# Attention of layers 1 to 3: the low parts of the turned probabilities before the maximum, and layer 2's queries in four pieces

## The chip, the cores and the metric

One core of one Trainium2 chip runs the whole program as one launch. The metric is the time of one execution in microseconds (us), the median of several runs. Engines are named as in the profile: PE (TensorE matmuls), PEld (its weight loads), DVE (VectorE), ACT (ScalarE), POOL (GpSimd), SP (SyncE).

## The reference, cut to what matters

The program is four layers of cross attention and a feed-forward network on x (1024 tokens of width 256, in 4 batches of 256) with a context of 4 x 512 keys of width 128. The change touches the attention of layers 1, 2 and 3 alone. Each has 16 heads of width 128. Of layer 1:

```python
q = (hidden_states @ Wq).reshape(B, Sq, H, D)
k = (encoder_hidden_states @ Wk).reshape(B, Skv, H, D)
v = (encoder_hidden_states @ Wv).reshape(B, Skv, H, D)
q = rmsnorm(q, gq)
k = rmsnorm(k, gk)
scores = jnp.einsum('bqhd,bkhd->bhqk', q, k) * scale
attn = jax.nn.softmax(scores, axis=-1)
out = jnp.einsum('bhqk,bkhd->bqhd', attn, v)
out = out.reshape(B, Sq, H * D)
return out @ Wo
```

Layers 2 and 3 are the same without the two norms; two heads share a key and a value head there, and a mask of the keys is applied. The result is added to x.

## The kernel before, in words

`heads_stage` (line 417) is called three times: "l1a" with `qk_norm` (layer 1), "l2a" with `made` (layer 2) and "l3a" (layer 3). Every product of full precision is made of three matmuls of fp32r operands: each operand is kept as a high part (rounded) and a low part (the difference), and high x high, high x low and low x high are added in PSUM (`product`, lines 565 to 569).

The head's weights are folded first: a = Wq Wk (so that the "queries" of a head are a times the normalised tokens, and the scores are those times the context), and wvo = Wv Wo. So each head is prepared in the pieces of `pieces` (line 435): "a", "q0" and "q1" (the queries of 512 tokens each, six matmuls of 512 columns) and "wvo". In layers 1 and 3, PE multiplies a and wvo too, and ACT copies them from a bank; in layer 2 (`made`) these products were made earlier and lie in SBUF, so that PE prepares q0 and q1 alone. ACT copies a piece out of its bank (line 669), POOL makes its high part (line 813) and its low part (line 817), from the second head on; for the first head ACT and DVE do it (lines 664 to 669 and 717).

The work of a head is four pairs, one for each batch; a pair is two units of 128 queries by 512 keys. There are 64 pairs in a layer. Each engine has its own queue in program order, and all of them go through `walk` (line 493): step k of an engine does one part each of several pairs. After the first head's preparation come eight steps written out, a hardware loop of six turns with eight steps each, eight more steps written out, and four steps that drain. In one step:

- PE: the scores of pair k (S: 6 matmuls of 512 columns, lines 608 to 620), the values of pair k-3 (V: 12 of 256 columns, lines 621 to 628), the output product of pair k-4 (Y: 6 of 256 columns, lines 629 to 640), one piece of the next head (`after`, line 641), then the turning of the probabilities of pair k-1 (T: 8 transposes, lines 643 to 650). In `walk` step k of a head prepares `pieces[k % 4]`, so a head's steps are: a, q0, q1, wvo.
- ACT: H, the high parts of pair k-2's turned probabilities, for its two units (line 676); E, the exponentials of pair k's two units with their sums (line 685); O, the high part of pair k-3's output (line 693 or 695); the copy of the piece (line 669).
- DVE: M, for each unit of pair k the mask (or the norm of the keys) with the maximum and the shift made of it (lines 732 to 748); the reciprocal of pair k-4's sums (line 753); L, the low parts of pair k-2's turned probabilities, two units (line 759); Olow, the low part of pair k-3's output (line 766 or 768); X, the two additions of pair k-4 to x (line 775).
- POOL: high and low parts of the next head's piece.
- SP loads weights in layers 1 and 3; in layer 2 it does nothing in the loop.

The banks: two for scores, two for turned probabilities (one per unit), one for the output, one for y, two for pieces. What sets the order around the change are these waits. H of a unit waits for T of that unit. L waits for H of the same unit (`high_done`). T of the next pair's unit waits for L (`turn_kept`), since it writes the same bank. E waits for M's shift (`shift_done`). O stands behind E in ACT's queue and waits for V. Olow waits for O (`o_high_done`). The next V waits for Olow (`o_kept`), and Y waits for X of the pair before (`x_added`), since each has one bank. X waits for Y. S of a unit waits for the maximum of the last pair's unit (`top_done`). The last steps of DVE's queue in one step, before:

```python
dve.reciprocal(inverse[:, at:at + 2], ...).then_inc(inverse_done, 1)
if exists(pair, 2):
    for q in range(2):
        dve.wait_ge(high_done, pair * 2 + (q - 3))
        dve.tensor_tensor(prob_low[part], turn_bank[q][:]..., prob_high[part]..., ALU.subtract).then_inc(turn_kept, 1)
if exists(pair, 3):
    dve.wait_ge(o_high_done, pair - 2)
```

Of the kernel before, what the change touches and what calls it, by code (L numbers as in the profile page):

```python
# [14 lines left out]
F32 = mybir.dt.float32  # L15
# [4 lines left out]
P = 128  # L20
BATCH = 4
# [395 lines left out]
def heads_stage(nc, m, dram, name, qk_norm, made=False):  # L417
# [16 lines left out]
    scale = float(P) ** -0.5  # L434
    pieces = ["a", "q0", "q1", "wvo"]
    n_pieces = len(pieces)
    on_bank = ["q0", "q1"] if made else pieces
    n_banked = len(on_bank)
    with Stage(nc, m, name) as st:
        if not made:  # L440
# [41 lines left out]
        if not qk_norm:  # L482
            norm.banks = turn_bank
        rms_loaded = st.sems("rms_loaded0", "rms_loaded1")
        (side_loaded, scores_ready, top_done, shift_done, exp_done, inverse_done, turn_ready,
         high_done, turn_kept, pv_ready, o_high_done, o_kept, own_high, split_done, y_ready, x_added, prep_ready,
# [3 lines left out]
            "x_added", "prep_ready", "prep_kept")  # L490
        set_up, gained, q_scale_done, first_high = st.sems("set_up", "gained", "q_scale_done", "first_high")

        def walk(engine, prepare, step, normalise=None):

            def two_heads(i, last=False):
                for k in range(2 * BATCH):
                    after, ahead = [pieces[k % BATCH]], k // BATCH + 1
                    if last and ahead == 2:  # L500
                        after = []
                    head = (i * 2 + k // BATCH, i, k // BATCH)
                    following = (i * 2 + ahead, i + ahead // 2, ahead % 2)
                    step(i * (2 * BATCH) + k, k, head, after, following)

            for piece in pieces:
                if piece == "q0" and normalise:
                    normalise(engine)
                prepare(piece, (0, 0, 0))
            two_heads(0)  # L510
            with engine.Fori(1, HEADS // 2 - 1) as i:
                two_heads(i)
            two_heads(HEADS // 2 - 1, True)
            for k in range(AHEAD):
                step(PAIRS + k, k, None, [], None)

        def is_head(h, number):
            return isinstance(h, int) and h == number

        parts_of = {"a": (a_high, a_low, a_h), "q0": (q_high, q_low, q_t), "q1": (q_high, q_low, q_t),  # L520
                    "wvo": (wvo_high, wvo_low, wvo)}

        def place(piece, slot):

            first, end = (int(piece[1]) * BANK, (int(piece[1]) + 1) * BANK) if piece in ("q0", "q1") else (0, D)
            return (slice(None), slot, slice(first, end)), end - first
# [7 lines left out]
        def exists(pair, back):  # L534

            return not isinstance(pair, int) or 0 <= pair - back < PAIRS

        with st.block() as block:
# [25 lines left out]
            def _(pe):  # L564
# [10 lines left out]
                def prepare(piece, head):  # L575
                    h, turn, slot = head
                    if piece not in on_bank:
                        return
                    n = on_bank.index(piece)
                    if piece == "a":  # L580
                        pe.wait_ge(w_loaded[slot], turn * 64 + 64)
                        if qk_norm:
                            pe.wait_ge(gained, h + 1)
                    bank = prep_bank[n % 2]
                    if is_head(h, 0):
                        wait_for(pe, split_done, 0 if made else n - 1)
                    elif is_head(h, 1) and n < 2:
                        pe.wait_ge(split_done, (2 if made else n_pieces - 1) + n)
# [17 lines left out]
                def step(pair, k, head, after, following):  # L606
# [22 lines left out]
                    if exists(pair, 4):  # L629
                        pe.wait_ge(o_kept, pair - 3)  # L630
                        wait_for(pe, x_added, pair * 2 - 8)
                        if k % BATCH == 0:
                            h = HEADS if head is None else head[0]
                            pe.wait_ge(split_done, h * n_pieces)
                        old = (k - 4) // BATCH % 2
# [4 lines left out]
                        last.then_inc(y_ready, 1)  # L640
                    for piece in after:
                        prepare(piece, following)
# [12 lines left out]
            def _(act):  # L655
# [14 lines left out]

                def step(pair, k, head, after, following):
                    if exists(pair, 2):
# [15 lines left out]
                    if exists(pair, 3):  # L688
# [8 lines left out]
                        last.then_inc(o_high_done, 1)  # L697
                    for piece in after:
                        prepare(piece, following)
# [4 lines left out]
            def _(dve):  # L704
                def prepare(piece, head):
                    h, turn, slot = head
                    if is_head(h, 0):
# [9 lines left out]
                        dve.tensor_tensor(low[at], of, high[at].bitcast(F32), ALU.subtract).then_inc(split_done, 1)  # L717

# [5 lines left out]

                def step(pair, k, head, after, following):
                    b = k % BATCH
                    if exists(pair, 0):
                        h, turn, slot = head
# [20 lines left out]
                    if exists(pair, 4):  # L749
# [37 lines left out]
            def _(pool):  # L787
# [9 lines left out]
                def prepare(piece, head):  # L797
                    h, turn, slot = head
                    if not is_head(h, 0):
                        number = h * n_pieces + pieces.index(piece)  # L800
                        high, low, whole = parts_of[piece]
                        at, _ = place(piece, slot)
                        if is_head(h, 1) and piece == "a":
                            pool.wait_ge(split_done, n_pieces)
                        if piece in on_bank:
# [6 lines left out]
                        pool.tensor_tensor(pool_woken[:], m.ones[:, 0:1], m.ones[:, 0:1], ALU.mult)  # L812
                        pool.tensor_copy(high[at], of).then_inc(own_high, 1)
                        pool.wait_ge(own_high, number + (1 - n_pieces))
                        if piece not in on_bank:
                            pool.tensor_tensor(second_woken[:], m.ones[:, 0:1], m.ones[:, 0:1], ALU.mult)
                        pool.tensor_tensor(low[at], of, high[at].bitcast(F32), ALU.subtract).then_inc(split_done, 1)
# [3 lines left out]
                def step(pair, k, head, after, following):  # L821
                    for piece in after:
                        prepare(piece, following)
# [2133 lines left out]
```

## Time and profile before

| | |
|---|---|
| median of 3 runs | 2414.33 us (2414.1 to 2418.16) |
| the profiled execution | 2415.74 us; its span is 2413.4 us |
| PE busy | 2119.8 us, 88% of the span |
| DVE busy | 1580.7 us, 65% |
| ACT busy | 1219.2 us, 51% |
| POOL busy | 777.2 us, 32% |
| mean granted TensorE clock | 0.913 of full speed |

The units of layer 1 run from 594.4 us of the span to 927.5, those of layer 2 from 1042.3 to 1370.9, those of layer 3 from 1829.4 to 2162.1 (first and last start of the operation of line 737); the drain of a layer follows. A busy share is a mean over stages with different limits; matmuls are pipelined, so that the durations of neighbouring ones overlap and their spacing is to be read from their starts. The profiled execution is 1.4 us above the median of the runs.

### The profile page before, as it was taken

How to read it: one execution, taken by the hardware profiler on the slowest of the kernel's cores; microseconds unless marked ns; L12 is line 12 of the kernel's file. 1: busy time of each engine (PE TensorE's matmuls, PEld its weight loads, DVE VectorE, ACT ScalarE, POOL GpSimd, SP SyncE). 2: the span in 40 equal slices, each digit the busy share in tenths (PEclk: the TensorE clock that was granted, in tenths of full speed). 3: DMA queues.
4: the chain of work that ended last, by engine and by line, in shares of the span. 5: the costliest groups of instructions: out<-in, count | busy, mean ns of one | idle time of the engine just before them, and what ended most of it. 6: DMA issues, size and time to landing. Idle time of an engine off the chain costs nothing. (4 is left out here: it accounts for less than half of the span.)

```text
span 2413.4 us, 42918 instructions
## 1 busy us (share of the span) xinstructions
PE 2119.8 (88%) x12471; PEld 1755.9 (73%) x12471; DVE 1580.7 (65%) x4466; ACT 1219.2 (51%) x3007; POOL 777.2 (32%) x1150
## 2 busy tenths in 40 slices
PE   5699978598999997789999978887868999996999
PEld 3555556476899995478888867777756999995887
DVE  6687858784777786577778863111236887885655
ACT  4788842274666664356666512222215666662333
POOL 3433312210333331123323156666632323311221
PEclk9777789799999998889999978998898999997999
DMA  1156020101211113100000026766761000004431
GB/s 62 43 112 188 0 88 1 64 2 44 73 72 60 60 66 106 39 4 1 0 0 0 5 82 195 204 203 188 210 218 32 16 20 20 20 1 109 118 110 50
DMA packets 132850, 174.01 MB, mean 72 GB/s; under 512 B 43820, under 2 KB 99092, under 8 KB 130040
## 3 DMA queue, kind: packets, MB, share of 16 engines
q1 hardware_dynamic: 121656, 140.27, 20.0%
q0 software_dynamic: 10656, 29.11, 3.9%
q10 hardware_dynamic: 416, 3.15, 0.3%
q8 instruction: 59, 0.97, 0.2%
q14 instruction: 63, 0.52, 0.1%
HBM read 155.57 MB, written 36.83 MB: 80 GB/s over the span
## 5 line engine op out<-in xcount | busy, mean ns | idle before, releaser
L2475 DVE COPY l2f_x_t<-bank 128x256 f32<-128x256 f32 x111 | 46.9, 424 | 269.3 <-PE bank L2205 132.2
L685 ACT ACTIVATE l1a_prob<-l1a_masked,l1a_shift,l1a_q_scale 128x512 f32<-128x512 f32 x128 | 104.4, 816 | 79.4 <-DVE l1a_shift L743 78.4
L2350 POOL DMA_INDIRECT l2f_x_rows_of<-l2f_x_rows,l2f_table x111 | 107.9, 972 | 88.9 <-remote 34.7
L2217 PE MATMUL bank<-l2f_x_t,l2f_w 128*128 128x128 f32 x888 | 128.4, 292 | 6.3 <-issue 6.0
L685 ACT ACTIVATE l2a_prob<-l2a_masked,l2a_shift 128x512 f32<-128x512 f32 x128 | 92.7, 724 | 81.1 <-DVE l2a_shift L747 78.3
L685 ACT ACTIVATE l3a_prob<-l3a_masked,l3a_shift 128x512 f32<-128x512 f32 x128 | 92.7, 724 | 80.3 <-DVE l3a_shift L747 77.6
L2306 ACT ACTIVATE l2f_h<-bank 128x128 f32<-128x128 f32 x111 | 30.8, 277 | 198.2 <-PE bank L2217 106.0
L2217 PEld LDWEIGHTS bank<-l2f_x_t,l2f_w 128*128 128x128 f32 x888 | 118.7, 208 | 9.2 <-issue 9.0
L2225 PE MATMUL bank<-l2f_w,l2f_h 128*128 128x256 f32 x222 | 77.1, 432 | 53.8 <-ACT l2f_h L2307 36.8
L1236 ACT ACTIVATE l0a_prob<-bank,l0a_shift 128x496 f32<-128x496 f32 (+1 forms) x256 | 122.6, 552 | 2.4 <-DVE l0a_shift L1260 2.3
L2355 POOL DMA_INDIRECT l2f_y_rows<-l2f_y,l2f_target x111 | 110.3, 994 | 37.5 <-issue 32.8
L1255 DVE TENSOR_REDUCE l0a_top<-bank 128x1 f32<-128x496 f32 (+1 forms) x256 | 90.2, 411 | 36.3 <-PE bank L1194 36.1
L737 DVE CUSTOM_DVE_ANT_0 l3a_masked<-bank,l3a_side 128x512 f32<-128x512 f32 x128 | 88.4, 691 | 18.0 <-issue 18.0
L737 DVE CUSTOM_DVE_ANT_0 l1a_masked<-bank,l1a_side 128x512 f32<-128x512 f32 x128 | 88.4, 691 | 15.0 <-issue 14.9
L737 DVE CUSTOM_DVE_ANT_0 l2a_masked<-bank,l2a_side 128x512 f32<-128x512 f32 x128 | 88.4, 691 | 12.6 <-issue 12.6
L2557 POOL TENSOR_TENSOR l3f_low<-l3f_raw,l3f_high 128x768 fp32r<-128x768 f32 x24 | 44.3, 1847 | 160.2 <-ACT l3f_high L2552 160.2
L1214 PEld LDWEIGHTS bank<-ident,l0a_prob 128*128 128x128 f32 x512 | 68.7, 167 | 30.5 <-issue 18.6
L1214 PE MATMUL bank<-ident,l0a_prob 128*128 128x128 f32 x512 | 87.8, 325 | 1.0 <-DVE l0a_prob L1269 0.3
L812 POOL TENSOR_TENSOR l3a_pool_woken<-ones 128x1 f32<-128x1 f32 x60 | 11.6, 193 | 231.2 <-ACT l3a_q_t L669 123.1
L2776 DVE TENSOR_TENSOR l3f_upped<-l3f_gate,bank 128x512 f32<-128x512 f32 x48 | 33.0, 688 | 77.7 <-PE bank L2677 69.7
L1194 PE MATMUL bank<-l0a_k_t,l0a_q_t 64*128 64x512 f32 x128 | 65.1, 567 | 21.1 <-ACT l0a_prob L1236 15.5
L812 POOL TENSOR_TENSOR l2a_pool_woken<-ones 128x1 f32<-128x1 f32 x60 | 11.6, 193 | 219.4 <-ACT l2a_q_t L669 183.3
(591 smaller groups left out, 7560.7 us busy)
## 6 DMA issues: line engine op xcount, KB each, us to landing
l2f_w<-w_rows SPq DMA_DIRECT2D x111, 304.0 KB
l1a_side<-rms SPq DMA_DIRECT2D x16, 1024.0 KB, 4.8
w_rows<-in_l2f_w SPq DMA_DIRECT2D x4, 2048.0 KB
l2f_hots<-l2f_y_rows SPq DMA_DIRECT2D x8, 768.0 KB, 10.0
l3f_raw<-in_l3f_w SPq DMA_DIRECT2D x24, 256.0 KB, 3.8
l3f_mix<-shares SPq DMA_DIRECT2D x16, 384.0 KB, 3.7
l2f_w_rest<-in_l2f_w SPq DMA_DIRECT2D x111, 48.0 KB
w_rows<-in_l2f_w SPq DMA_DIRECT2D x8, 512.0 KB
```

The lines of the kernel that those rows point to most:

```text
L685: act.activation(prob[:, unit, :], masked[:, unit, :], ACT.Exp, bias=shift[:, unit:unit + 1], scale=q_scale[:, slot, t:t + 1] if qk_norm e ...
L737: dve.tensor_tensor_reduce(masked[:, unit, :], score_bank[q][:], side[:, slot if qk_norm else 0, b * KEYS:(b + 1) * KEYS], 1.0, LOWEST, AL ...
L1194: pe.matmul(score_bank[k % 2 * 2 + q][:], q_t[rows, slot, q * P:(q + 1) * P], k_t[rows, slot, :], start=True, stop=True).then_inc(scores_r ...
L1214: last = pe.transpose(turn_bank[q][:, n * P:(n + 1) * P], prob[:, (k - 3) % 4, q, n * P:(n + 1) * P], m.ident[:])
L1236: last = act.activation(prob[:, at, q, first:end], score_bank[at % 2 * 2 + q][:, first:end], ACT.Exp, bias=shift[:, at, q, part:part + 1], ...
L1255: last = dve.tensor_reduce(top[:, at, q, part:part + 1], score_bank[k % 2 * 2 + q][:, first:end], AX_X, ALU.max)
L2217: last = pe.matmul(pair_bank[b % 2][:, n * P:(n + 1) * P], w[:, slot, first:first + P], x_t[:, b % 2, c * P:(c + 1) * P], start=(c == 0), ...
L2225: pe.matmul(y_bank[b % 2][:, 0:D], h[:, b % 2, 0, :], w[:, slot, DC * of.WIDTH:of.ROW], start=True, stop=False)
L2350: pool.indirect_dma_start(x_rows_of[:, b % of.X_SLOTS, :], None, x_rows, bass.IndirectOffsetOnAxis(table[:, b:b + 1], 0)).then_inc(gathere ...
L2355: pool.indirect_dma_start(y_rows, bass.IndirectOffsetOnAxis(target[:, b:b + 1], 0), y[:, b % of.Y_SLOTS, :], None).then_inc(y_stored[b % o ...
L2475: dve.tensor_copy(x_t[:, b % 2, :], turn_bank[b % 2][:, 0:D]).then_inc(x_kept, 1)
L2557: pool.tensor_tensor(self.low[:, slot, at], self.raw[:, slot, at], self.high[:, slot, at].bitcast(F32), ALU.subtract).then_inc(self.low_do ...
```

## The change

It does two things, in `heads_stage` alone.

1. All three layers: in DVE's step, L (lines 755 to 760) moves from behind the reciprocal to the head of the step, before M. So DVE's order is L, M, reciprocal, Olow, X. The queues of the other engines keep their order.
2. Layer 2 alone: the queries of a head are made in four pieces of 256 tokens (q0 to q3, each six matmuls of 256 columns), one in each of the head's four steps, in place of two of 512 in the middle two. wvo comes behind q3 in the fourth step, and "a" of the head after the next behind that, on POOL; "a" has its own semaphores (`a_done`, `own_a`). Before the first step "a" of head 1 is prepared too. PE's scores wait for the quarter that they read.

```diff
-    pieces = ["a", "q0", "q1", "wvo"]
+    queries = ["q0", "q1", "q2", "q3"] if made else ["q0", "q1"]
+    per_query = TOKENS // len(queries)
+    pieces = ["a"] + queries + ["wvo"]
     n_pieces = len(pieces)
-    on_bank = ["q0", "q1"] if made else pieces
+    on_bank = queries if made else pieces
+    due = [["q0"], ["q1"], ["q2"], ["q3", "wvo"]] if made else [[piece] for piece in pieces]
     n_banked = len(on_bank)
+    n_split = n_pieces - 1 if made else n_pieces
...
                 for k in range(2 * BATCH):
-                    after, ahead = [pieces[k % BATCH]], k // BATCH + 1
-                    if last and ahead == 2:
-                        after = []
+                    ahead = k // BATCH + 1
                     head = (i * 2 + k // BATCH, i, k // BATCH)
                     following = (i * 2 + ahead, i + ahead // 2, ahead % 2)
-                    step(i * (2 * BATCH) + k, k, head, after, following)
+                    after = [] if last and ahead == 2 else [(piece, following) for piece in due[k % BATCH]]
+                    if made and k % BATCH == BATCH - 1 and not last:
+                        after.append(("a", (i * 2 + ahead + 1, i + (ahead + 1) // 2, (ahead + 1) % 2)))
+                    step(i * (2 * BATCH) + k, k, head, after)
...
                 prepare(piece, (0, 0, 0))
+            if made:
+                prepare("a", (1, 0, 1))
...
-                    elif piece in ("q0", "q1"):
+                    elif piece in queries:
                         chunk = int(piece[1])
-                        pe.wait_ge(split_done, h * n_pieces + 1)
+                        if made:
+                            pe.wait_ge(a_done, h + 1)
+                        else:
+                            pe.wait_ge(split_done, h * n_pieces + 1)
                         for c in range(DC):
-                            last = product(bank[:], [of[:, slot, c * P:(c + 1) * P] for of in (a_high, a_low)],
-                                           [of[:, c, chunk * BANK:(chunk + 1) * BANK] for of in (m.x_high, m.x_low)],
+                            last = product(bank[:, 0:per_query], [of[:, slot, c * P:(c + 1) * P] for of in (a_high, a_low)],
+                                           [of[:, c, chunk * per_query:(chunk + 1) * per_query] for of in (m.x_high, m.x_low)],
                                            c == 0, c == DC - 1)
...
-                        if b % 2 == 0:
+                        if made:
+                            pe.wait_ge(split_done, h * n_split + (b + 1))
+                        elif b % 2 == 0:
                             pe.wait_ge(split_done, h * n_pieces + (2 + b // 2))
...
                     b = k % BATCH
+                    if exists(pair, 2):
+                        for q in range(2):
+                            dve.wait_ge(high_done, pair * 2 + (q - 3))
+                            part = (slice(None), k % 2, slice(None), slice(q * P, (q + 1) * P))
+                            dve.tensor_tensor(prob_low[part], turn_bank[q][:].rearrange("p (n t) -> p n t", n=KT),
+                                              prob_high[part].bitcast(F32), ALU.subtract).then_inc(turn_kept, 1)
                     if exists(pair, 0):
...
                         dve.reciprocal(inverse[:, at:at + 2], total[:, (k - 4) % 8 * 2:(k - 4) % 8 * 2 + 2]
                                        ).then_inc(inverse_done, 1)
-                    if exists(pair, 2):
-                        for q in range(2):
-                            dve.wait_ge(high_done, pair * 2 + (q - 3))
-                            part = (slice(None), k % 2, slice(None), slice(q * P, (q + 1) * P))
-                            dve.tensor_tensor(prob_low[part], turn_bank[q][:].rearrange("p (n t) -> p n t", n=KT),
-                                              prob_high[part].bitcast(F32), ALU.subtract).then_inc(turn_kept, 1)
...
                     if not is_head(h, 0):
-                        number = h * n_pieces + pieces.index(piece)
+                        if made and piece == "a":
+                            own, done, number = own_a, a_done, h
+                        else:
+                            own, done, number = own_high, split_done, h * n_split + (pieces.index(piece) - (n_pieces - n_split))
```

## Rows read from the trace of the kernel before

**Rows 1.** The page, busy time and share of the span.
```profile
PE 2119.8 (88%) x12471; PEld 1755.9 (73%) x12471; DVE 1580.7 (65%) x4466; ACT 1219.2 (51%) x3007; POOL 777.2 (32%) x1150
```

**Rows 2.** Windows: us; busy PE, PEld, DVE, ACT, POOL; clock, DMA share, GB/s.
```profile
640.00:880.00 240.00, 239.81 (x1635) 217.01 (x1635) 192.26 (x626) 158.43 (x359) 78.05 (x155) 1.00 0.19 66
1090.00:1330.00 240.00, 236.35 (x1564) 207.89 (x1563) 192.51 (x625) 149.75 (x337) 75.33 (x156) 1.00 0.00 0
```

**Rows 3.** Line 736, two per pair: three loops, layer 2's last pairs.
```profile
L736 DVE MEMSET l1a_woken<- x97: 59/59/59, 634.1 to 891.6; 128x1 f32 x97
L736 DVE MEMSET l2a_woken<- x97: 59/59/59, 1077.7 to 1335.6; 128x1 f32 x97
L736 DVE MEMSET l3a_woken<- x97: 59/59/59, 1869.0 to 2126.0; 128x1 f32 x97
L736 DVE MEMSET l2a_woken<- x15: 59/59/59, 1335.6 to 1370.0; 128x1 f32 x15
```

**Rows 4.** Timeline, layer 2, PE: start us, duration us. A pair with queries.
```profile
1194.90 0.48 PE L567 MATMUL bank<-ctx_t_high,l2a_q_high 128*128 128x512 f32 x1
...
1196.37 0.28 PE L567 MATMUL bank<-l2a_prob_high,ctx_high 128*128 128x256 f32 x1
...
1198.49 0.39 PE L567 MATMUL bank<-l2n_x_high,l2a_a_high 128*128 128x512 f32 x1
...
1199.89 1.04 PE L648 MATMUL bank<-ident,l2a_prob 128*128 128x128 f32 x8
...
1200.68 0.48 PE L567 MATMUL bank<-ctx_t_high,l2a_q_high 128*128 128x512 f32 x1
```

**Rows 5.** Timeline, layer 2, PE: the start of the second pair without queries.
```profile
1205.83 0.50 PE L567 MATMUL bank<-ctx_t_high,l2a_q_high 128*128 128x512 f32 x1
```

**Rows 6.** Timeline, layer 2, DVE and ACT, the step that starts at 1190.22 us.
```profile
1190.22 0.06 DVE L736 MEMSET l2a_woken<- 128x1 f32 x1 [0.39 <-PE bank L569]
...
1192.18 0.72 ACT L685 ACTIVATE l2a_prob<-l2a_masked,l2a_shift 128x512 f32<-128x512 f32 x1 [0.18 <-DVE l2a_shift L747]
...
1192.26 1.27 DVE L759 TENSOR_TENSOR l2a_prob_low<-bank,l2a_prob_high 128x512 fp32r<-128x512 f32 x2
...
1192.90 0.46 ACT L695 ACTIVATE l2a_o_high<-bank,l2a_valid 128x256 fp32r<-128x256 f32 x1
...
1193.44 0.47 DVE L768 SCALAR_TENSOR_TENSOR l2a_o_low<-bank,l2a_valid,l2a_o_high 128x256 fp32r<-128x256 f32 x1
...
1193.84 0.86 DVE L776 SCALAR_TENSOR_TENSOR x<-bank,l2a_inverse,x 128x256 f32<-128x256 f32 x2
...
1194.31 0.59 ACT L669 COPY l2a_q_t<-bank 128x512 f32<-128x512 f32 x1 [0.95 <-PE bank L569]
...
1194.79 1.08 ACT L676 CAST l2a_prob_high<-bank 128x512 fp32r<-128x512 f32 x2
```

**Rows 7.** Timeline, layer 1, DVE and ACT, the step that starts at 703.27 us.
```profile
703.27 0.06 DVE L736 MEMSET l1a_woken<- 128x1 f32 x1 [0.46 <-PE bank L569]
...
706.05 0.35 ACT L693 CAST l1a_o_high<-bank 128x256 fp32r<-128x256 f32 x1
...
706.82 0.86 DVE L776 SCALAR_TENSOR_TENSOR x<-bank,l1a_inverse,x 128x256 f32<-128x256 f32 x2
```

**Rows 8.** Timeline, layer 2, DVE and ACT, a step written out, then the drain.
```profile
1365.43 0.69 DVE L737 CUSTOM_DVE_ANT_0 l2a_masked<-bank,l2a_side 128x512 f32<-128x512 f32 x1 [0.28 <-issue]
...
1367.95 0.46 ACT L695 ACTIVATE l2a_o_high<-bank,l2a_valid 128x256 fp32r<-128x256 f32 x1
...
1375.32 0.47 ACT L695 ACTIVATE l2a_o_high<-bank,l2a_valid 128x256 fp32r<-128x256 f32 x1 [0.88 <-PE bank L569]
...
1375.83 0.48 DVE L768 SCALAR_TENSOR_TENSOR l2a_o_low<-bank,l2a_valid,l2a_o_high 128x256 fp32r<-128x256 f32 x1 [0.29 <-ACT l2a_o_high L695]
```

**Rows 9.** Timeline, layer 2, POOL: the first of wvo, the last of a.
```profile
1204.51 0.19 POOL L812 TENSOR_TENSOR l2a_pool_woken<-ones 128x1 f32<-128x1 f32 x1 [1.65 <-PE bank L569]
...
1206.70 0.74 POOL L817 TENSOR_TENSOR l2a_a_low<-products,l2a_a_high 128x256 fp32r<-128x256 f32 x1
```

More of the change, by code:

```diff
@@ L490, in heads_stage @@
             "x_added", "prep_ready", "prep_kept")
-        set_up, gained, q_scale_done, first_high = st.sems("set_up", "gained", "q_scale_done", "first_high")
+        set_up, gained, q_scale_done, first_high, a_done = st.sems("set_up", "gained", "q_scale_done", "first_high", "a_done")
         def walk(engine, prepare, step, normalise=None):
@@ L514, in walk @@
             for k in range(AHEAD):
-                step(PAIRS + k, k, None, [], None)
+                step(PAIRS + k, k, None, [])
         def is_head(h, number):
             return isinstance(h, int) and h == number
-        parts_of = {"a": (a_high, a_low, a_h), "q0": (q_high, q_low, q_t), "q1": (q_high, q_low, q_t),
-                    "wvo": (wvo_high, wvo_low, wvo)}
+        parts_of = {"a": (a_high, a_low, a_h), "wvo": (wvo_high, wvo_low, wvo)} | {q: (q_high, q_low, q_t) for q in queries}
         def place(piece, slot):
-            first, end = (int(piece[1]) * BANK, (int(piece[1]) + 1) * BANK) if piece in ("q0", "q1") else (0, D)
+            first, end = (int(piece[1]) * per_query, (int(piece[1]) + 1) * per_query) if piece in queries else (0, D)
             return (slice(None), slot, slice(first, end)), end - first
@@ L585, in prepare @@
                     if is_head(h, 0):
-                        wait_for(pe, split_done, 0 if made else n - 1)
+                        wait_for(pe, split_done, n - 1)
                     elif is_head(h, 1) and n < 2:
-                        pe.wait_ge(split_done, (2 if made else n_pieces - 1) + n)
+                        pe.wait_ge(split_done, n_banked - 1 + n)
                     else:
@@ L604, in prepare, with step @@
                     last.then_inc(prep_ready, 1)
-                def step(pair, k, head, after, following):
+                def step(pair, k, head, after):
                     b = k % BATCH
@@ L640, in step @@
                         last.then_inc(y_ready, 1)
-                    for piece in after:
+                    for piece, following in after:
                         prepare(piece, following)
@@ L669, in prepare, with step @@
                     act.copy((high if is_head(h, 0) else whole)[at], bank[:, 0:width]).then_inc(prep_kept, 1)
-                def step(pair, k, head, after, following):
+                def step(pair, k, head, after):
                     if exists(pair, 2):
@@ L697, in step @@
                         last.then_inc(o_high_done, 1)
-                    for piece in after:
+                    for piece, following in after:
                         prepare(piece, following)
@@ L716, in prepare @@
                             of = of_products(piece, h)
-                        dve.tensor_tensor(low[at], of, high[at].bitcast(F32), ALU.subtract).then_inc(split_done, 1)
+                        dve.tensor_tensor(low[at], of, high[at].bitcast(F32), ALU.subtract).then_inc(
+                            a_done if made and piece == "a" else split_done, 1)
                 def set_up_masks(dve):
@@ L723, in set_up_masks, with step @@
                                       ALU.max).then_inc(set_up, 1)
-                def step(pair, k, head, after, following):
+                def step(pair, k, head, after):
                     b = k % BATCH
+                    if exists(pair, 2):
[4 more added lines that the diff above has]
+                                              prob_high[part].bitcast(F32), ALU.subtract).then_inc(turn_kept, 1)
                     if exists(pair, 0):
@@ L799, in prepare @@
                     if not is_head(h, 0):
-                        number = h * n_pieces + pieces.index(piece)
+                        if made and piece == "a":
+                            own, done, number = own_a, a_done, h
+                        else:
+                            own, done, number = own_high, split_done, h * n_split + (pieces.index(piece) - (n_pieces - n_split))
                         high, low, whole = parts_of[piece]
                         at, _ = place(piece, slot)
-                        if is_head(h, 1) and piece == "a":
-                            pool.wait_ge(split_done, n_pieces)
+                        if is_head(h, 1) and piece == ("q0" if made else "a"):
+                            pool.wait_ge(split_done, n_split)
+                        if is_head(h, 1) and piece == "a" and made:
+                            pool.wait_ge(a_done, 1)
                         if piece in on_bank:
@@ L812, in prepare, with step @@
                         pool.tensor_tensor(pool_woken[:], m.ones[:, 0:1], m.ones[:, 0:1], ALU.mult)
-                        pool.tensor_copy(high[at], of).then_inc(own_high, 1)
-                        pool.wait_ge(own_high, number + (1 - n_pieces))
+                        pool.tensor_copy(high[at], of).then_inc(own, 1)
+                        pool.wait_ge(own, number if made and piece == "a" else number + (1 - n_split))
                         if piece not in on_bank:
                             pool.tensor_tensor(second_woken[:], m.ones[:, 0:1], m.ones[:, 0:1], ALU.mult)
-                        pool.tensor_tensor(low[at], of, high[at].bitcast(F32), ALU.subtract).then_inc(split_done, 1)
+                        pool.tensor_tensor(low[at], of, high[at].bitcast(F32), ALU.subtract).then_inc(done, 1)
                     if qk_norm and piece == "wvo" and not is_head(h, HEADS - 1):
                         gain_weights(h + 1, turn + slot, 1 - slot)
-                def step(pair, k, head, after, following):
-                    for piece in after:
+                def step(pair, k, head, after):
+                    for piece, following in after:
                         prepare(piece, following)
```

3 lines of the change are left out of this document (2 added, 1 removed).

## The prediction

> **What bounds the kernel now.** The page comes first: PE is busy for 88% of the span, more than any other engine [rows 1], but that is a mean over many stages, so I cut out two stretches of the changed stage. In layer 1 PE is busy for 239.81 of 240 us; in layer 2 for 236.35 of 240, DVE for 192.51 and ACT for 149.75 [rows 2], with the granted clock at 1.00, the upper of PE's two levels (2.4 GHz), throughout. So layers 1 and 3 are PE's, and layer 2 is PE's with 3.65 us per 240 left open. The spacing of line 736 gives the pace: 48 pairs take 257.5, 257.9 and 257.0 us in the loops of layers 1, 2 and 3, that is 5.365, 5.373 and 5.354 us a pair, and the last seven spacings of layer 2 take 34.4 us, 4.91 each [rows 3].
>
> PE's queue says what a pair must cost in layer 2. S takes 1.47 us, V and Y together 2.12 (18 matmuls of 256 columns, 0.118 each), Q, six matmuls of 512 columns, 1.40 (0.233 each), T 0.79: 5.78 with queries [rows 4], 4.38 without. The pair without queries that starts at 1200.68 takes 5.15 [rows 4, 5], since there T waits for L, and L stands behind M. That ring (S, M, L, T, S) is what the change takes away, and the spread of the queries evens the load: (2 x 5.78 + 2 x 4.38) / 4 = 5.08 us of PE a pair. Were PE the bound, this would be the pace of layer 2.
>
> **Part 1, L moved ahead of M: what it uncovers.** Nothing is added; every DVE operation stays, so what counts is what each stood beside. In the step at 1190.22 DVE's M ends where the second E starts, 1192.18 (E is released by the shift); E runs 0.72, and O starts as it ends, 1192.90, back to back: ACT's queue holds O behind E. O ends at 1193.36, Olow starts at 1193.44, and L stood from 1192.26 to 1193.44 exactly in this gap [rows 6]. So L's 1.18 us was free: DVE had work while ACT made E and O. After the change nothing but the reciprocal lies between M and Olow. DVE must wait for E and O in every step, and L is paid in front. This is a new ring inside one step, on two queues in program order: L, M, E, O, Olow, X, then the next step's L.
>
> Its length in layer 2's loop, by [rows 6]: L 1.18 (1192.26 to 1193.44); M with the second E and O up to O's end 3.14 (1190.22 to 1193.36); DVE's start after O 0.04 (in the drain, where Olow waits alone, O ends at 1375.79 and Olow starts at 1375.83 [rows 8]); Olow 0.40; X 0.86. The sum is 5.62. Where one DVE operation follows another directly they overlap by some 0.09 (L would end at 1193.53, Olow starts at 1193.44), and X before L is such a seam: 5.53 to 5.62, and I take 5.58, layer 3 alike. In layer 1 O is shorter: 703.27 to O's end at 706.40 is 3.13, plus 0.04; Olow and X end at 707.68, and X starts at 706.82, so X is 0.86; Olow to X I take as 0.33 to 0.40; with L 1.18 that is 5.54 to 5.61, less the seam: 5.45 to 5.61, and I take 5.51, as Olow has no scale there [rows 7]. In the steps written out M and E are closer: 1365.43 to 1368.41 is 2.98, against 3.14; ring 5.44, layer 1 5.37 [rows 8].
>
> Does anything else lengthen it? PE: V of the next pair waits for Olow, so it can start 0.9 before X ends. PE then needs 1.40 for V, 0.71 for Y, at most 1.40 for Q and 0.79 for T, so T ends about 3.5 us after L's start, while H, which waits for T, stands behind O on ACT at 4.4: not late. S is ready some 2 us before M asks for it. A pair with queries needs 5.78 on PE, 0.2 to 0.3 over the ring; two in a row slip by 0.6 at most, which that slack covers, and the pairs without queries give it back. ACT: after O it copies the piece (0.48 to its successor) and runs the first H (0.54), 1.02 in all, against 1.26 of Olow and X on DVE [rows 6], so L finds H done. So the ring sets the pace alone, and it is longer than the mean pace of all three layers.
>
> Sum of part 1 and the loops: layer 1 (5.51 - 5.365) x 48 = 7.0; layer 2 (5.58 - 5.373) x 48 = 9.9; layer 3 (5.58 - 5.354) x 48 = 10.8. The last seven spacings: layer 2 7 x 5.44 - 34.4 = 3.7; the others, whose last steps carry the same pairs, an estimate of 2.5 and 2.9. The first eight: O and X are only just coming in, and four full spacings at 5.44 stand against about 5.3; with L's first delay of M (under 1.2, I take 0.8) that is 1.0, 1.8 and 1.3. Together 40.9.
>
> **Part 2, four quarters in layer 2.** PE's columns stay the same: 24 matmuls of 256 columns a head at 0.118 are 2.83 us, 12 of 512 at 0.233 are 2.80 [rows 4]. So I cost the cut at nothing, and beneath the ring PE has 0.5 us a pair open besides. The Trainium skill, TensorE: Matmul & The Clock Gate, section "Back-to-back issue gap", speaks against the cut: it gives a sustained spacing of about 81 ns at 128 columns and 131 ns at 512, which between them makes some 98 ns at 256 (an estimate from that page), so that a head's 24 would cost 2.35 us and the 12 only 1.57, 0.8 more a head and 12 us in the layer, if PE bounds. The rows of 0.233 and 0.118 do not bear it out: here the cost goes by the column. ACT and POOL have two more fixed costs a head, both beside slack. At the start DVE's masks stand in front of the first quarter's low part, and two more pieces follow through two banks: bounded by nothing and by two pieces of 0.7, I take 0.8.
>
> One new wait: "a" now follows q3 and wvo on POOL, and PE's first quarter of the next step waits for it. wvo and a take 2.93 us (1204.51 to 1207.44 [rows 9]), a quarter half of that, so a is done 4.4 us after ACT's copy. In the ring's time that is about 3.5 into the next step, where PE would like it at 1.3: PE stands 2 us, T ends near 5, and the first H starts about when ACT is free. I cost it at nothing, at most 0.3 x 15 = 4.5.
>
> **Sum.** 40.9 + 0.8 = 41.7. The profiled execution took 2415.74, of which the span is 2413.4, so it would take 2457; it stands 1.4 over the median of the runs, 2414.33, and from that I predict 2456.
>
> **The rivals.**
>
> *PE stays the bound, and it gets faster.* If the step's ring were under 5.08, the old ring's loss in layer 2 would be gained: (5.373 - 5.08) x 48 = 14, with the ends 15, and layers 1 and 3, where PE has no gap, stay: 2399. For it: PE's shares [rows 2], and that T no longer waits for L. Against it: E and O leave Olow no way past them, and the ring would have to lose 0.5 us. It decides at a ring of 5.37, which is 0.21 below mine. Chance 0.05.
>
> *It comes out even.* A ring near 5.37, so that both sides cancel to within 0.2% of the time (5 us, about what a measurement can tell from no change here): the seams between operations would have to be three times what I see. Chance 0.04.
>
> *Lockstep.* PE's slips are not given back: V waits for Olow and M for S, so that each pair costs the larger of PE and the ring. Then 28 pairs with queries in layer 1 and 28 in layer 3, at 5.78, add 0.27 x 28 + 0.20 x 28 = 13; the loop's turns, and POOL's "a", another 5 each at most: 2470 to 2480. For it: one bank each for output and y. Against it: the slack counted above. Chance 0.15.
>
> *The forecast,* the ring alone, 0.76. Slower by over 0.2% holds forecast and lockstep: 0.91. The range: the ring at its lower ends, 0.06 a pair over 180 pairs, is 11 us less, and a little for ends that cost nothing: 2440. At the top it takes in lockstep and POOL's wait: 2480.
>
> **What the profile after would show.** Right: DVE idle before Olow by 1.1 to 1.2 us in nearly every step, released by ACT's O, 180 times, over 200 us in all; L with no long wait; PE in the two stretches down to 220 to 230 of 240 busy; pairs in the loop all of 5.5 to 5.6, with queries or without; line 736 over 48 pairs at 264 to 268 us. The stages outside unchanged. Step by step: M to O's end unchanged at 3.1; in layer 2 PE waits for POOL's a_low once a head. Wrong: if pairs alternate between 5.8 and 5.5, it is lockstep; if Olow starts with no wait, the ring is not closed and the time is PE's, under 2414; if L waits for H, the ring goes through T and is longer than mine.

## The result, and the profile after

The changed kernel takes 2451.49 us (median of 4 runs, 2450.26 to 2455.01) against 2416.24 for the kernel before in the same measurement (2414.1 to 2423.45): a ratio of 1.0147, 95% interval 1.0128 to 1.0165. It is 35 us slower; forecast were 42 (2456, in a range of 2440 to 2480). The profiled execution took 2455.01 us, its span 2453.2.

The page and two stretches inside layers 1 and 2 (columns as in [rows 2]):

```profile
PE 2126.9 (87%) x12663; PEld 1777.4 (72%) x12663; DVE 1575.9 (64%) x4468; ACT 1199.8 (49%) x3039; POOL 797.8 (33%) x1240
...
660.00:900.00 240.00, 237.91 (x1614) 215.06 (x1613) 188.25 (x620) 152.62 (x354) 79.44 (x157) 1.00 0.18 65
1120.00:1360.00 240.00, 228.07 (x1659) 211.62 (x1659) 188.03 (x611) 143.39 (x350) 86.09 (x220) 1.00 0.00 0
```

PE, which filled layer 1 before, now leaves 2.1 us of 240 open there and 11.9 in layer 2, against 0.2 and 3.65 [rows 2]; DVE is less busy too (188 of 240 against 192). In layer 2 no engine is full any more: that is the sign of a ring, of waits that pass the turn round. In layer 1 the busy share says little, as PE's rows still cover 99% of the stretch; there it is the count of matmuls in 240 us, 1614 against 1635, and the spacing below that show the loss. The granted clock stayed at 1.00, the upper level.

The same line as in [rows 3] (it is line 755 now), two per pair, over the 48 pairs of each loop and layer 2's last seven spacings:

```profile
L755 DVE MEMSET l1a_woken<- x97: 59/59/59, 634.8 to 895.4; 128x1 f32 x97
L755 DVE MEMSET l2a_woken<- x97: 59/59/59, 1090.0 to 1353.7; 128x1 f32 x97
L755 DVE MEMSET l3a_woken<- x97: 59/59/59, 1898.3 to 2161.8; 128x1 f32 x97
L755 DVE MEMSET l2a_woken<- x15: 59/59/59, 1353.7 to 1391.6; 128x1 f32 x15
```

260.6, 263.7 and 263.5 us: 5.43, 5.49 and 5.49 a pair, against 5.365, 5.373 and 5.354 before. A pair no longer takes 4.9 or 5.8 us as it prepares queries or not; all take the same. The last seven of layer 2 take 37.9 us against 34.4.

One step of layer 2's loop, DVE and ACT, in order of time (start us, duration us); it answers to [rows 6]:

```profile
1132.71 1.28 DVE L744 TENSOR_TENSOR l2a_prob_low<-bank,l2a_prob_high 128x512 fp32r<-128x512 f32 x2
...
1133.91 0.69 DVE L756 CUSTOM_DVE_ANT_0 l2a_masked<-bank,l2a_side 128x512 f32<-128x512 f32 x1
...
1135.80 0.17 DVE L772 RECIPROCAL l2a_inverse<-l2a_total 128x2 f32<-128x2 f32 x1
1135.80 0.72 ACT L697 ACTIVATE l2a_prob<-l2a_masked,l2a_shift 128x512 f32<-128x512 f32 x1
...
1136.52 0.45 ACT L707 ACTIVATE l2a_o_high<-bank,l2a_valid 128x256 fp32r<-128x256 f32 x1
...
1137.01 0.48 DVE L781 SCALAR_TENSOR_TENSOR l2a_o_low<-bank,l2a_valid,l2a_o_high 128x256 fp32r<-128x256 f32 x1 [1.05 <-ACT l2a_o_high L707]
1137.41 0.87 DVE L789 SCALAR_TENSOR_TENSOR x<-bank,l2a_inverse,x 128x256 f32<-128x256 f32 x2
...
1138.20 1.29 DVE L744 TENSOR_TENSOR l2a_prob_low<-bank,l2a_prob_high 128x512 fp32r<-128x512 f32 x2
```

L now stands at the head, and behind the reciprocal DVE is idle for 1.05 us until ACT's O is done; the next L starts 5.49 us after the last. The waits of DVE before Olow in the whole of layer 2 (us, times), from the view of the tile l2a_o_low:

```profile
  ACT l2a_o_high L707: 68.2, 64
```

64 times in 64 pairs; layers 1 and 3 show 66.9 and 67.1 us, so 202 us in all, where [rows 6] had L.

And the longest waits of layer 2's stretch from 1120 to 1360 us (who waited for whom: us in all, times, longest):

```profile
POOL l2a_pool_woken L830 <- ACT l2a_q_t L681: 150.4, 44, 4.1
ACT l2a_prob L697 <- DVE l2a_shift L766: 91.3, 71, 2.2
DVE l2a_o_low L781 <- ACT l2a_o_high L707: 46.2, 44, 1.2
...
PE bank L574 <- ACT l2a_q_t L681: 7.6, 11, 0.7
PEld bank L574 <- POOL l2a_a_low L835: 5.8, 10, 0.6
PE bank L574 <- POOL l2a_a_low L835: 4.4, 11, 0.6
```

ACT waits for M's shift, DVE for ACT's O: the two sides of the ring. The last rows are two waits of PE once a head, the one for POOL's a, which was foreseen, and one for ACT's copy of the last quarter, which was not; the experiments come back to both.

### The profile page after: what moved, and what is told of

It reads as the page before. It is cut to its first block and busy times, and to the rows that moved or that the text cites. A ratio compares the mean times of both kernels' runs of the same rounds, so it can differ in the third digit from the quotient of the medians.

```text
span 2453.2 us, 43857 instructions
## 1 busy us (share of the span) xinstructions
PE 2126.9 (87%) x12663; PEld 1777.4 (72%) x12663; DVE 1575.9 (64%) x4468; ACT 1199.8 (49%) x3039; POOL 797.8 (33%) x1240
## 5 line engine op out<-in xcount | busy, mean ns | idle before, releaser
L1273 DVE TENSOR_REDUCE l0a_top<-bank 128x1 f32<-128x496 f32 (+1 forms) x256 | 90.3, 412 | 35.5 <-PE bank L1212 35.3
L830 POOL TENSOR_TENSOR l2a_pool_woken<-ones 128x1 f32<-128x1 f32 x90 | 18.5, 206 | 214.7 <-ACT l2a_q_t L681 207.8
L744 DVE TENSOR_TENSOR l1a_prob_low<-bank,l1a_prob_high 128x512 fp32r<-128x512 f32 x128 | 82.0, 683 | 7.7 <-ACT l1a_prob_high L688 7.5
L744 DVE TENSOR_TENSOR l3a_prob_low<-bank,l3a_prob_high 128x512 fp32r<-128x512 f32 x128 | 82.0, 683 | 6.8 <-ACT l3a_prob_high L688 6.8
```

Of the source, the lines that this page charges most:

```text
L1273: last = dve.tensor_reduce(top[:, at, q, part:part + 1], score_bank[k % 2 * 2 + q][:, first:end], AX_X, ALU.max)
```

## The experiments

Every ratio is to the kernel before, run in turn on the same chip. The kernels low_first_alone, quarters_alone, after_low_split and after_o_first ran beside a kernel before of 2415 us, the other six, in two later sets of runs, beside one of 2359 us. It is not the chip: one chip gave 2415.15 in the first set and 2359.41 in the last, and another gave 2359.27. The difference lies between layers 2 and 3, outside the changed stages: from layer 2's last M to layer 3's first it is 404 us in before_pad, 459 in the profile of before. So I compare ratios and the loops, not times. In the diffs, "-" is the changed kernel unless said otherwise.

### Each part alone

**low_first_alone** is the kernel before with the first part of the change only:

```diff
                 def step(pair, k, head, after, following):
                     b = k % BATCH
+                    if exists(pair, 2):
+                        for q in range(2):
...
                     if exists(pair, 0):
...
-                    if exists(pair, 2):
-                        for q in range(2):
```

> Part 1 alone: L before M in all three layers, layer 2's queries in halves as before. The ring (L, M, E, O, Olow, X, 5.42 to 5.49 us a pair in the changed kernel) sets the pace whether the queries come in halves or quarters, so the loops of 48 pairs stay at about 260.5, 263.7 and 263.5 us; only layer 2's start, which took some 3 us longer with quarters, comes back. Ratio to before 1.013, 1.0147 less 3 of 2416. The rival, that the cut into quarters carries the loss in layer 2: that layer's loop back at 258 us or under and the ratio at 1.009 or below.

Measured: 1.013 (1.0101 to 1.016), the loops at 260.6, 263.4 and 263.4 us: the ring theory's numbers to a few tenths. Halves or quarters, layer 2 runs at the same 5.49. Its start (from the first product of queries to the first M) takes 6.9 us against 8.7, so 1.8 came back and not 3; the part on the terms below says why.

```profile
L742 DVE MEMSET l2a_woken<- x97: 59/59/59, 1091.6 to 1355.0; 128x1 f32 x97
```

**quarters_alone** is the changed kernel with L put back behind the reciprocal:

```diff
-                    if exists(pair, 2):
-                        for q in range(2):
...
                         dve.reciprocal(...)
+                    if exists(pair, 2):
+                        for q in range(2):
```

> Part 2 alone: the quarters in layer 2, L behind the reciprocal as before. The ring theory: PE bounds at 5.08 us a pair in layer 2, plus what PE waits for POOL's a, some 0.6 us a head, so 5.2 a pair and 250 to 252 us for the loop's 48 pairs against 257.9; layers 1 and 3 as before; layer 2's start 3 us longer. In all 4 to 6 us faster than before, ratio 0.998. The rival, that a matmul of 256 columns costs more than half of one of 512: 5.28 or more a pair and no gain. The rival that quarters are the loss: slower than before.

Measured: 0.9979 (0.9964 to 0.9993), layer 2's loop at 252.4 us, 5.26 a pair, a little over the 252 expected; 257.5 and 256.9 in the other layers, as before. So the whole loss is part 1's, and part 2 alone is a gain. The two do not add up to the change (1.013 times 0.998 would be 1.011, against 1.0147, a difference at the edge of the intervals). The loops show it more surely: with the ring in force layer 2's loop takes 263.4 us with halves and 263.7 with quarters, so its pace does not hear of PE's evener load. Its PE rows where a head begins (start us, duration us, idle before):

```profile
1166.40 0.28 PE L576 MATMUL bank<-l2a_wvo_high,l2a_o_low 128*128 128x256 f32 x1
1167.03 0.39 PE L574 MATMUL bank<-l2n_x_high,l2a_a_high 128*128 128x256 f32 x1 [0.35 <-POOL l2a_a_low L835]
1167.25 0.28 PE L575 MATMUL bank<-l2n_x_low,l2a_a_high 128*128 128x256 f32 x1
1167.37 0.28 PE L576 MATMUL bank<-l2n_x_high,l2a_a_low 128*128 128x256 f32 x1
```

From the second on a quarter's matmuls start 0.12 us apart, as [rows 4] had it for 256 columns. But the first comes 0.63 after the last of Y, where 0.12 is usual, and waits for POOL's a: one pair in four takes 5.7 us, the others 5.0 to 5.16.

### What the ring is made of

**after_pad** and **before_pad** put one more operation on ACT, between the second E and O, into the changed kernel and into the one before; **after_pad_behind** puts it behind O. The added work (a copy of a constant that nothing reads) leaves the computation as it is.

```diff
                     if exists(pair, 3):
+                        act.copy(pad[:, k % 4, :], m.ident[:])
                         act.wait_ge(pv_ready, pair - 2)
...
                         last.then_inc(o_high_done, 1)
+                        act.copy(pad[:, k % 4, :], m.ident[:])
```

(The first line stands in after_pad and before_pad, the second in after_pad_behind.)

> The changed kernel with one more ACT operation in each step between the second E and O: a copy of the 128x128 identity into a buffer that nothing reads, 0.18 to 0.25 us by its neighbours. The ring theory: it lies on the ring, every pair gets longer by its whole length, 5.49 to about 5.7, so 35 to 47 us in 190 pairs; ratio 1.029 to 1.034. If ACT's idle time (over 40% of the layer) could take it, the ratio would stay at 1.0147.

> The same added copy at the same place in the kernel before. There L stands beside E and O and PE is the bound, so it should cost next to nothing: ratio 1.000 to 1.003. If any work between E and O costs its length in either kernel, 1.015 or more.

> The same added copy in the changed kernel, but behind O. It is off the ring through Olow and X; it stands on the branch to H, which has some 0.2 to 0.4 us of slack before L, so most of it hides: ratio 1.0147 to 1.019, with the loop of layer 2 at 263.7 us as before. If the place behind E counts and not the ring, the same 1.029 to 1.034 as with the copy ahead of O.

Measured: after_pad 1.0297 (1.0281 to 1.0313), before_pad 0.9996 (0.9987 to 1.0005), after_pad_behind 1.0172 (1.0156 to 1.0188). The copy holds ACT for 0.19 us:

```profile
1200.61 0.28 ACT L702 COPY l2a_pad<-ident 128x128 f32<-128x128 f32 x1
1200.80 0.47 ACT L709 ACTIVATE l2a_o_high<-bank,l2a_valid 128x256 fp32r<-128x256 f32 x1
```

and after_pad's loops are longer by 9.1, 9.2 and 9.4 us, 0.19 in each of the 48 pairs:

```profile
L757 DVE MEMSET l1a_woken<- x97: 59/59/59, 635.7 to 905.3; 128x1 f32 x97
L757 DVE MEMSET l2a_woken<- x97: 59/59/59, 1101.4 to 1374.3; 128x1 f32 x97
```

So the same instruction at the same place costs its full length in one kernel and nothing in the other. Behind O it costs 0.25% in place of 1.5%: layer 3's loop stays (263.3 us), layers 1 and 2 take 2.1 and 2.2 us more, where I had expected layer 2's to stay too. So the ring and the branch (ACT's work behind O: the copy of the piece, then H, for which the next L waits) are told apart, and the branch has some slack, not much.

Where the 2.2 us of layer 2 fall, the trace shows: its pairs take 5.49 as before, but one in four takes 5.70. In that step PE's quarter has waited for POOL's a, so ACT's copy of it comes late, H behind the copy, and L behind H (after_pad_behind, ACT and DVE):

```profile
1114.46 0.29 ACT L711 COPY l2a_pad<-ident 128x128 f32<-128x128 f32 x1
...
1114.92 0.37 ACT L682 COPY l2a_q_t<-bank 128x256 f32<-128x256 f32 x1 [0.17 <-PE bank L577]
...
1115.36 1.07 ACT L689 CAST l2a_prob_high<-bank 128x512 fp32r<-128x512 f32 x2
...
1115.98 0.69 DVE L746 TENSOR_TENSOR l2a_prob_low<-bank,l2a_prob_high 128x512 fp32r<-128x512 f32 x1
```

The first H ends at 1115.95 and L starts at 1115.98. In layer 1 it is the two pairs in four that copy 512 columns (0.58 us, against 0.37 for 256) that get longer, to 5.48 and 5.53 to 5.63 from 5.42 and 5.45. Layer 3 copies the same pieces, but its ring is 0.06 longer, and there the branch just fits in: H ends 0.06 us before L starts.

### Breaking the ring

**after_low_split** leaves L's first unit ahead of M and puts the second behind the reciprocal:

```diff
-                        for q in range(2):
+                        for q in (0,):
                             dve.wait_ge(high_done, pair * 2 + (q - 3))
...
                         dve.reciprocal(...)
+                    if exists(pair, 2):
+                        for q in (1,):
+                            dve.wait_ge(high_done, pair * 2 + (q - 3))
...
```

> The changed kernel with the low part of the first unit kept ahead of M and that of the second moved back behind the reciprocal. The ring loses one half of L, 0.61 of 5.49, and is 4.88, under what PE needs (5.08 in layer 2, 5.3 in 1 and 3), and the gap before Olow holds the other half: ratio 0.994 to 1.000, DVE's idle before Olow down by about 0.6 a pair. If the loss were not a ring but some mean of work put late, half of it would stay: ratio 1.007.

Measured: 0.9948 (0.9928 to 0.9968), loops 255.3, 252.5 and 254.6 us: faster than both kernels. PE has no gap left in layer 1. The page's columns of [rows 2] for it:

```profile
660.00:900.00 240.00, 240.00 (x1646) 219.24 (x1645) 194.26 (x631) 158.94 (x360) 80.33 (x157) 1.00 0.19 65
1120.00:1340.00 220.00, 216.19 (x1591) 202.92 (x1592) 183.09 (x588) 143.50 (x334) 80.74 (x206) 1.00 0.00 0
```

**after_o_first** moves O ahead of the two E in ACT's step:

```diff
+                    if exists(pair, 3):
+                        act.wait_ge(pv_ready, pair - 2)
...
                     if exists(pair, 0):
                         h, _, slot = head
...
-                    if exists(pair, 3):
-                        act.wait_ge(pv_ready, pair - 2)
```

> The changed kernel with one thing moved: in ACT's step O stands before the two E in place of behind them. The ring theory: Olow no longer waits for E, DVE's idle before Olow goes from over 1 us to nearly nothing, and PE bounds again: layers 1 and 3 at or a little under their times before (5.31 to 5.36 a pair), layer 2 near 5.2, so in all 2400 to 2412 us, ratio 0.993 to 0.999. The rival, that M's later place is the loss (E and so the next T come later) and not O's place behind E: E gets later still here, so the time stays at 2440 or above.

Measured: 1.0051 (1.0036 to 1.0067), a miss. Two thirds of the loss are gone, and nearly all of DVE's wait before Olow with them, but the rest was not where I expected it: loops 263.5, 256.6 and 261.6 us. Layer 1 takes 22.0 us a head where PE's own work is 21.24 (after_low_split, in which PE has no gap there, takes 21.27). The trace shows the difference in one place, 0.77 us, the first scores of a head (layer 1, PE and ACT):

```profile
719.11 1.04 PE L660 MATMUL bank<-ident,l1a_prob 128*128 128x128 f32 x8
...
720.04 0.35 ACT L681 COPY l1a_wvo<-bank 128x256 f32<-128x256 f32 x1
...
720.67 0.50 PE L574 MATMUL bank<-ctx_t_high,l1a_q_high 128*128 128x512 f32 x1 [0.53 <-ACT l1a_wvo L681]
```

The turning that starts at 719.11 needs 0.79 and is done at 719.9, yet the scores start at 720.67, released by ACT's copy of wvo (720.04 to 720.39). The scores of a head's first pair wait until ACT has copied all pieces. That copy stands behind E, and E now stands behind O, which waits for V. The move opened one ring and made a longer way through another wait: that was my reading, and the next run tests it. **o_first_free** takes that wait out (the scores still wait for the low parts of what they read) and makes layer 2's a early ("-" is after_o_first here):

```diff
-                    if made and k % BATCH == BATCH - 1 and not last:
+                    if made and k % BATCH == 1 and not last:
...
-                        if b == 0:
-                            pe.wait_ge(prep_kept, h * n_banked + n_banked)
```

> The changed kernel with O before E (ratio 1.0051) and two waits opened: a of layer 2 made early, as in the run before, and the scores of a head's first pair no longer wait for ACT's copies of all its pieces (they wait for the pieces' low parts in any case). With O before E, O waits for V, and E and the copy of the piece stand behind it; the next head's scores then wait for that copy, 0.8 us a head in layer 1 (21.24 us of PE work a head, 22.0 measured). If that is what kept the kernel at 1.005, PE bounds everywhere now: 5.31, 5.1 and 5.31 us a pair, ratio 0.988 to 0.992. If it is a second ring through H and L, it stays over 1.000.

Measured: 0.989 (0.9874 to 0.9907); loops 255.1, 244.2 and 254.4 us. Now PE is the bound in every stretch:

```profile
660.00:900.00 240.00, 240.00 (x1649) 219.33 (x1649) 191.60 (x636) 152.52 (x362) 80.30 (x157) 1.00 0.18 65
1120.00:1300.00 180.00, 180.00 (x1348) 170.88 (x1347) 152.22 (x497) 109.32 (x281) 69.29 (x178) 1.00 0.00 0
```

240.00 of 240 and 180.00 of 180 us. DVE still waits for H ahead of L there (42.4 us in the stretch of layer 1, 48.2 in after_o_first), at PE's full pace: that is slack and no second ring. Layer 1 shows the wait by itself, since a early touches layer 2 alone: its 63 spacings take 329.4 us against 340.9.

**low_split_a_early** and **low_split_free** add the same two edits one after the other to the split kernel:

> The kernel with L split around M (ratio 0.9948) with one thing more: in layer 2, a of the head after the next is made in the second step of a head and not behind q3 and wvo in the fourth. The theory that PE waits 0.6 us a head for POOL's a (5.70 in place of 5.09 us for that pair): this wait goes, 15 x 0.6 = 9 us less, ratio 0.991. If the longer pair had another cause (the wait of the scores for ACT's copy of q3), it stays at 0.995.

> L split around M, a early, and the scores' wait for the copies left out. In the split kernel T and S follow each other without a gap in every pair, so the wait for the copies should be worth nothing: the same as with a early alone, 0.991. A gain of over 0.2% beyond it would say that the copy was on the path there too.

Measured: 0.9922 (0.9908 to 0.9935) and 0.9909 (0.9892 to 0.9925), against 0.9948 for the split alone. Layer 2's loop goes from 252.5 to 245.0 us with a early, and PE's wait for a_low is gone from the list. Taking out the scores' wait for the copies brings the loop to 244.1 and no more than the intervals allow. The two fastest kernels, low_split_free and o_first_free, are not told apart by their intervals (their medians are 2339.67 and 2332.97 us, with runs that overlap); both beat the kernel before by about 1% and the changed one by over 2%.

Layer 2's loop in low_split_a_early and in low_split_free:

```profile
L755 DVE MEMSET l2a_woken<- x97: 59/59/59, 1072.4 to 1317.4; 128x1 f32 x97
L753 DVE MEMSET l2a_woken<- x97: 59/59/59, 1073.9 to 1318.0; 128x1 f32 x97
```

## Why the prediction was right, and by how much its terms were off

The mechanism was right. L had been free beside E and O, and at the head of the step it closes the ring L, M, E, O, Olow, X on two queues. after_pad and before_pad show that E and O are on the path in one kernel and not in the other; after_low_split shows that half of L, put back, opens it; low_first_alone and quarters_alone show that part 1 is the whole loss and part 2 a gain. Of the rivals, "PE stays the bound" failed as said (it needed a ring under 5.37), "it comes out even" too (it needed one near 5.37; layer 1's 5.43 came closest), and lockstep did not come: layer 1's pairs with queries, 5.78 of PE's work, take 5.42 by DVE's pace like the others.

That the number came so near is in part luck. Four groups of terms stood for 41.7 us, and their errors went both ways: the three loops 27.7 predicted against 15.3 measured, the first eight spacings 4.1 against 7.2, the last seven 9.1 against 8.7, layer 2's start 0.8 against 2.7. Of the signs that I had named, DVE's wait before Olow came as said (1.05 to 1.07 us, 192 times, 202 us in all), but the loops stayed under the 264 to 268 us, and PE in layer 1 did not fall to 220 to 230 of 240: it stayed at 237.9.

**The ring was sized 0.08 to 0.09 too long.** I took 5.51, 5.58 and 5.58; it is 5.43, 5.49 and 5.49. By the step shown above: L to M 1.22 (I had 1.18), the start of line 755 (1133.93) to O's end 3.04 (3.14), Olow's start after O 0.04 (0.04), Olow 0.40 (0.40), X to L 0.79 (0.86). M's part of it: before, its first operation waited for PE at every step, and the second unit's came 0.99 after it; now it follows L directly, and the second unit's follows 0.91 after the first. The rest is the seam from X to L, 0.07 where I had allowed 0 to 0.09 and taken about half. These hundredths weigh much, as the loss is only what the ring has over PE's pace: I took 0.145, 0.207 and 0.226 a pair, and it is 0.065, 0.120 and 0.135, about half. By layer the loops lost 3.1, 5.7 and 6.5 us.

**The starts were sized too short.** The first eight spacings cost 2.0, 3.1 and 2.1 us (I had 1.0, 1.8 and 1.3); the last seven 2.5, 3.6 and 2.6 (2.5, 3.7, 2.9: right). From layer 2's first product of queries to its first M it takes 8.7 us against 6.0, so the start costs 2.7, not 0.8: all four quarters run at the lower level of PE's clock (granted clock 0.50, 1.2 GHz), their matmuls 0.21 apart, where I had priced them at 0.118. The window over them, and the one in low_split_a_early, which has the same quarters but gets the upper level before the third and needs 6.8 us:

```profile
1043.00:1049.00 6.00, 5.33 (x24) 5.04 (x24) 4.10 (x5) 1.12 (x3) 2.08 (x4) 0.50 0.00 0
```

```profile
1031.00:1036.00 5.00, 4.33 (x24) 3.85 (x24) 3.85 (x5) 1.12 (x3) 2.02 (x4) 0.74 0.00 0
```

PE stood still between the second and third quarter in both, 0.67 us, waiting for a low part of DVE's; which of the two a program gets is not settled here. And the clock varied with the halves too. The profile of before got the upper level after six of its twelve matmuls; in low_first_alone and before_pad, with the same halves, all twelve ran at the lower level, 0.43 apart (0.39 at the last in low_first_alone), and they need 6.9 and 7.2 us:

```profile
1047.10:1054.00 6.90, 6.22 (x16) 4.65 (x17) 4.92 (x6) 2.23 (x4) 0.00 (x0) 0.66 0.01 2
```

```profile
1035.20:1042.40 7.20, 6.53 (x17) 4.65 (x18) 4.95 (x7) 2.29 (x4) 0.00 (x0) 0.59 0.01 2
```

So of the 2.7 us the cut into quarters makes up 0.7 (6.75 in low_split_a_early against 6.02 in before, both reaching the upper level half way) to 1.5 (8.68 in the changed kernel against 7.17 in before_pad, both at the lower level throughout the queries); the rest is the clock that the two profiles happened to get. The 0.8 that I gave was near the first, and that is also why low_first_alone won back 1.8 us and not 3.

The sum of all these is 33.8 us; the medians differ by 35.3, the two profiled executions by 39. Of what is left in the profiles, 5.6 us lie between layers 2 and 3, where the kernel is unchanged.

**POOL's a** was foreseen with its order and its place: it is done 3.4 us after the start of the next L (I had 3.5). But PE is ready for it at 2.9 and not at 1.3, so it stands 0.5 us, not 2. In the changed kernel that costs next to nothing, as the ring covers it (the pairs of layer 2 are all 5.49 to 5.52). Once the ring is open it costs 0.6 us a head: 7.5 us of layer 2's loop between the split kernel and the one with a early. **The cut** into quarters cost PE nothing where the clock was at its upper level. The rule that I cited for the opposite (the Trainium skill, TensorE: Matmul & The Clock Gate, section "Back-to-back issue gap") would have made the quarters 0.8 us a head dearer; the trace does not agree: six matmuls of 256 columns take 0.71 us, and o_first_free's layer 2 runs at 5.09 a pair, which is PE's own sum with 0.118 each, 5.08.

What stays open: what sets the level of PE's clock at layer 2's start, and why M's two units stand closer when L comes directly before them.

## What to carry to other kernels

Before an operation is moved forward in an in-order queue, ask what it stood beside. If the engine fell in two halves around a round trip to another engine, the operation was its cover; moving it puts its own length on the ring, and what the ring then has over the old bound is lost in every turn (here L's 1.2 us made the ring 5.49, and 0.06 to 0.13 us a pair was lost), even if the engine looks idle for a fifth of the time. Add up the ring through both queues and compare it with the bound's own work per turn; and then look for the wait that becomes the next ring, here a wait for more than the reader needs.

## What was not expected of the hardware

M's two units started 0.99 us apart in layer 2's loop before (1.02 in layer 1's), where the first waited for PE ([rows 6] show that wait), and start 0.90 to 0.91 apart where it follows L directly, with the same instructions. The same split holds in the other runs: 0.99 to 1.02 in quarters_alone and before_pad, which kept the wait, 0.90 to 0.96 in all the others (medians of the loops). Over 190 pairs the 0.08 is 15 us. Whether the wait is the cause was not tried by itself.

And the same kernel before took 2415 us in one set of runs and 2359 in a later one on the same chip, while the loops of before_pad (257.6, 257.9 and 257.0 us) are those of before in [rows 3] to 0.1 us. Between layers 2 and 3, where the difference lies, both traces move the same 76.90 MB by DMA, at 183 GB/s in before (from 1400 to 1820 us) and at 208 in before_pad (from 1400 to 1770). What made the transfers slower is not shown.
